# Transposed chunks loaded and split ahead of the tail, the rank ahead of the weight split, low halves of expert weights in two pieces

## What is computed

```python
x = _layernorm(x + attention(x))             # 16 heads, causal
scores = x @ gate_w.T; probs = softmax(scores)
_, idx = top_k(probs + gate_b, 6)            # of E = 16 experts
for each expert:                              # H = 176
    h = silu(x @ W1.T + B1) * (x @ W3.T + B3)
    y += c[:, None] * (h @ W2.T + B2)         # c: prob, 0 if not chosen
z = silu(x @ ws1.T + bs1) * (x @ ws3.T + bs3) @ ws2.T + bs2   # shared, HS = 352
x = _layernorm(x + y + z)
```

## Time and profile before

| | us |
|---|---|
| median of 3 runs | 1126.18 (1124.87 to 1127.89) |
| the profiled execution | 1117.81 |
| its span, first to last instruction | 1115.7 |
| PE busy | 1033.5 (93%) |
| DVE busy | 759.2 (68%) |
| POOL busy | 738.6 (66%) |
| ACT busy | 674.3 (60%) |

### The profile page before, as it was taken

One profiled execution on the slowest core, in us unless ns is written; L12 is line 12 of the kernel. 1 busy time (PEld: TensorE's weight loads), 2 busy tenths in 40 slices (PEclk: granted clock), 3 DMA queues, 4 the chain that ended last, 5 costly groups with the idle time before them and its releaser, 6 DMA issues.

```text
span 1115.7 us, 28318 instructions
## 1 busy us (share of the span) xinstructions
PE 1033.5 (93%) x8028; PEld 845.6 (76%) x8029; DVE 759.2 (68%) x2406; ACT 674.3 (60%) x1680; POOL 738.6 (66%) x671
## 2 busy tenths in 40 slices
PE   7899998989999997798988999999999999999993
PEld 4546564646555553478988999999999999999993
DVE  8786878786878787668756555555555555555467
ACT  3567676767676765755545555555555555555546
POOL 4223368887888888866725666666666666666667
PEclk9999999999999999989999999999999999999997
DMA  6624254545454635466957666777776777777686
GB/s 186 184 75 115 77 141 149 166 143 159 139 172 134 180 128 163 147 214 218 293 162 165 110 117 121 117 117 118 118 120 113 119 119 117 118 117 121 114 238 237
DMA packets 127036, 163.53 MB, mean 147 GB/s; under 512 B 18800, under 2 KB 107504, under 8 KB 126704
## 3 DMA queue, kind: packets, MB, share of 16 engines
q1 hardware_dynamic: 82240, 99.73, 31.0%
q0 software_dynamic: 39024, 54.29, 27.6%
q10 hardware_dynamic: 5696, 8.55, 2.5%
HBM read 65.36 MB, written 73.85 MB: 125 GB/s over the span
## 4 chain that ended last, share of the span: by engine, by line
PE 74%; DVE 12%; ACT 4%; issue 4%; DMA 3%; POOL 2%; SPq 1%; ACTq 0%; POOLq 0%; DVEq 0%
PE psum L1061 18%; PE psum L1088 13%; PE psum L796 10%; PE psum L838 5%; PE psum L826 5%; PE psum L811 4%; PE psum L1046 4%; PE psum L1072 4%; PE psum L1057 3%; DVE rowmax L1501 3%; ACT probs L1164 2%; PE psum L1027 2%; PE psum L813 2%; PE psum L870 1%; DMA stack_q<-shift_l 1%
## 5 line engine op out<-in xcount | busy, mean ns | idle before, releaser
L1164 ACT ACTIVATE probs<-psum 128x512 f32<-128x512 f32 (+2 forms) x384 | 186.4, 529 | 115.8 <-PE psum L826 113.6
L1501 DVE TENSOR_REDUCE rowmax<-psum 128x1 f32<-128x512 f32 (+3 forms) x352 | 212.5, 633 | 60.5 <-PE psum L813 58.1
L2030 POOL DMA_INDIRECT xs_d<-x1p,index x192 | 204.5, 1065 | 52.5 <-issue 45.3
L2098 POOL DMA_INDIRECT x_d<-y_sb,tokens x104 | 162.9, 1566 | 98.6 <-ACT y_sb L1358 48.6
L2098 POOL DMA_INDIRECT z_d<-y_sb,tokens x103 | 161.2, 1565 | 81.4 <-issue 39.4
L1840 DVE TENSOR_TENSOR xb_lo<-psum,xb_hi 128x256 fp32r<-128x256 f32 x207 | 87.9, 425 | 186.2 <-ACT xb_hi L1155 186.2
L1061 PE MATMUL psum<-we_hi_lo,xb_hi 128*128 x828 | 200.6, 323 | 0.0
L1088 PE MATMUL psum<-we_hi_lo,hb_hi 88*128 (+1 forms) x828 | 174.6, 304 | 0.0
L1358 ACT ACTIVATE y_sb<-psum,combine 128x256 f32<-128x256 f32 x207 | 98.4, 475 | 125.0 <-PE psum L1088 112.4
L811 PE MATMUL psum<-stack_k,stack_q 96*128 96x256 bf16 (+3 forms) x512 | 139.0, 311 | 10.9 <-DVE rowmax L1501 4.8
L1061 PEld LDWEIGHTS psum<-we_hi_lo,xb_hi 128*128 128x128 f32 x828 | 146.6, 189 | 0.1
(11 more groups left out here) (206 smaller groups left out, 2326.4 us busy)
## 6 DMA issues: line engine op xcount, KB each, us to landing
xb<-xs_d SPq DMA_DIRECT2D x207, 138.0 KB
stack_q<-q_h SPq DMA_DIRECT2D x48, 128.0 KB
stack_k<-k_h SPq DMA_DIRECT2D x45, 128.0 KB
w_raw<-in_we SPq DMA_DIRECT2D x9, 608.0 KB, 4.4
xT_raw<-in_xT SPq DMA_DIRECT2D x9, 512.0 KB
stack_q<-q_m SPq DMA_DIRECT2D x32, 128.0 KB
stack_k<-k_m SPq DMA_DIRECT2D x32, 128.0 KB
x_res<-in_x SPq DMA_DIRECT2D x8, 512.0 KB, 3.7
```

The lines of the kernel that those rows point to most:

```text
L1164: nc.scalar.activation(probs[kt][:, heads[0]:heads[0] + n, :], st[f % ST_BANKS][:, 0:n * width].rearrange("p (h t) -> p h t", h=n), ACT.Ex ...
L1501: nc.vector.reduce_max(rowmax[gpar][:, heads[0]:heads[0] + n, qt], src, AX.X).then_inc(sm_free, 1)
L2030: nc.gpsimd.indirect_dma_start(out=xs_d[:, :], out_offset=bass.IndirectOffsetOnAxis(ap=index[tp][:, n:n + 1], axis=0), in_=x1p[tp][:, n // ...
L2098: nc.gpsimd.indirect_dma_start(out=(x1_d, z_d)[k % 2][:, :], out_offset=bass.IndirectOffsetOnAxis(ap=tokens[:, k:k + 1], axis=0), in_=y_sb ...
```

## The change

- `W_BY_HALVES_FROM = 6`: from tile 6 on, the low half of an expert is no longer made in its tile T ahead of the epilogue, but in two subtractions of 608 columns, behind the epilogues of tiles T + 1 and T + 2. The rank of tile 12 and the router parts of tile 9 thereby stand ahead of it on DVE. `wt_lo` counts with the second piece.
- Three of the four late chunks (12 to 14) are loaded in blocks 20, 22 and 23, into the memory of `late_raw` and of the first tiles' `hidden`, `h_hi`, `h_lo`, after SP has waited for the last late low half. So a third turn is unrolled (`LATE_TURNS = 3`). Chunk 15 is loaded behind the loop, between the first loads of z and those of x1.
- The late chunks have a buffer each for their halves (`X1T_tail`), and are split at tiles 32, 33, 34 and 38, without a wait for PE. The tail has its own `hidden`, `h_hi`, `h_lo` (`tail_h`), in memory of the first experts.
- `FINAL_FROM = T1 + 6`, `SUMS_AHEAD = 4`: statistics of unit m two tiles sooner, four sums ahead.

```diff
-LATE_TURNS = 2
+LATE_TURNS = 3
...
-FINAL_FROM, SUMS_AHEAD = T1 + 8, 3
+FINAL_FROM, SUMS_AHEAD = T1 + 6, 4
...
+X1T_LATE_AT = {20: 0, 22: 1, 23: 2}
+X1T_SPLIT_AT = {2: 0, 3: 1, 4: 2, 8: 3, 9: 4}
+W_BY_HALVES_FROM = 6
...
+        x1T_late = [sb(f"x1T_late{n}", [P, KD, HT_TOK], where=phase_x) for n in range(len(X1T_LATE_AT))]
+        phase_x.close()
...
+        tail_h = [[sb(f"tail_{name}{n}", [P, HT_TOK], dt) for n in range(2)]
+                  for name, dt in (("hidden", fp32), ("h_hi", f32r), ("h_lo", f32r))]
+        x1T_late += [sb(f"x1T_late{n}", [P, KD, HT_TOK]) for n in range(len(X1T_LATE_AT), HALVES - HC1 - 2)]
...
+        X1T_tail = [sb(f"x1T_tail{n}", [P, 2, KD, HT_TOK], f32r) for n in range(HALVES - HC1 - 2)]
...
+            if T >= T1 + 2:
+                hc = HC1 + 2 + X1T_SPLIT_AT.get(T - T1, HALVES)
+                return hc if hc < HALVES else None
...
-                    if last and k < len(x1T_late):
-                        load_x1T(HC1 + 2 + k)
+                    if isinstance(j0, int) and j0 + k in X1T_LATE_AT:
+                        sp.wait_ge(late_w_lo, 2 * LATE_W)
+                        load_x1T(HC1 + 2 + X1T_LATE_AT[j0 + k])
...
+                if n == 1:
+                    for hc in range(HC1 + 2 + len(X1T_LATE_AT), HALVES):
+                        load_x1T(hc)
...
-                if hc >= 2 and hc != HC1 + 1:
+                if 2 <= hc <= HC1:
                     act.wait_ge(uv_tile_full, ST * (hc - 1))
...
+            def split_half_w(i, half):
+
+                e, cols = W_ORDER[i - ST], slice(half * W_COLS // 2, (half + 1) * W_COLS // 2)
+                if half == 0:
+                    dve.wait_ge(wt_hi, i + 1)
+                last = nc.vector.tensor_tensor(w_all[:, e, 1, cols], w_raw[i % 2][:, cols],
+                                               w_all[:, e, 0, cols].bitcast(fp32), ALU.subtract)
+                if half == 1:
+                    last.then_inc(wt_lo, 1)
...
-                if T in W_ITEM_AT:
+                if T in W_ITEM_AT and T < W_BY_HALVES_FROM:
                     split_w(W_ITEM_AT[T])
...
                 epilogue(T)
+                for half in range(2):
+                    if T - 1 - half in W_ITEM_AT and T - 1 - half >= W_BY_HALVES_FROM:
+                        split_half_w(W_ITEM_AT[T - 1 - half], half)
```

More of the change, by code:

```diff
@@ L244, in postln_layer @@
     phase_a = ExitStack()
-    phase_b, phase_w, phase_z, phase_l = ExitStack(), ExitStack(), ExitStack(), ExitStack()
+    phase_b, phase_w, phase_z, phase_l, phase_x = [ExitStack() for _ in range(5)]
     def sem(name):
@@ L1008, in shared_up @@
                     pe.wait_ge(hidden_done, T - 1)
-                src = X1T[hc % 2]
+                src = x1_halves(hc)
                 for i in range(2):
```

33 lines of the change are left out of this document (17 added, 16 removed).

## The result

The changed kernel takes 1129.54 us in the median of 20 runs (1121.71 to 1138.33), the kernel before 1123.47 us in the median of its 20 beside them (1115.72 to 1127.89). The ratio is 1.0044 with a 95% interval of 1.0026 to 1.0062: **slower by 5 to 6 us**, where 5.3 us faster had been forecast.

What follows compares the result with a forecast made beforehand. TensorE, 74% of the chain, was taken as full inside the loop, leaving three joints: -2.0 - 0.6 - 2.7 = -5.3 us, profiled 1117.81 to 1112.5, plus 8.4 to the median: 1120.9 us, own range 1118.5 to 1123.

Steps and rivals of the forecast that it cites:

- Joint one: Way into the block loop: rank before the weight split 1.8 us, shorter scatters 0.2; -2.0 us, bounds -0.8 and -2.8.
- the loads that wait for the low halves stay covered: Entry: next expert's raw weights load two tiles later, each due three tiles behind the last low half; no cost.
- rival (b): Entry: the loop's start does not move because another wait ends last there; 1122.9 us, chance 0.13.
- the lock: Entry: whole VectorE subtractions hold up GpSimd's scatters, so halving them could bring the entry up to -2.8 us.
- Joint two: Inside the block loop: late loads moved to blocks 20, 22, 23; -0.9 and +0.3, together -0.6 us, bounds -1.1 and +0.6.
- Rival (a): Loop and tail: add backlog not relieved, early statistics eat their gain; tail -0.5, loop +0.3, 1124.0 us, chance 0.20.
- The zero for the unrolled turn: Block loop: saves a loop edge of about 0.1 us, fetches new instructions; 0, bounds -0.2 and +0.6.
- the one for SyncE's wait: Block loop, block 21: SyncE's new wait for late low halves is covered with margin 1.1 us, cost 0.
- Joint three: Way out of the loop, statistics from tile 36 instead of 38: -3.5 + 0.3 + 1.6 - 1.1 = -2.7 us, bounds -4.0 and +0.5.
- -1.1: Tail: TensorE loses its stalls for x1 low halves since every chunk has its own buffer; bounds -0.5 and -1.3 us.
- +0.3 for tiles 46 and 47: Tail: two adds and their statistics moved there bring VectorE to about a tile's length; costs 0.3 us.
- rival (c): Tail: slower, the tile-36 wait lengthened by three loads before the first x1 chunk; tail +3.0, 1127.5 us, chance 0.07.

Runs made afterwards that it cites:

- d_turn: Kernel before with only the third turn of eight blocks unrolled, nothing loaded in it: 0.9991 (0.9961 to 1.0022), median 1120.46 against 1123.01.
- e_order: Kernel before with the rank ahead of the weight split, low half whole in its own tile right behind the rank: 0.9975 (0.9944 to 1.0006).
- w_later: Kernel before with the rank first and the low half whole, two tiles later: 0.9990 (0.9968 to 1.0013).
- u_loads: Changed kernel with only two turns unrolled and the three late-chunk loads back in the last blocks: 1.0018 (0.9994 to 1.0042) against the kernel before.
- d_entry_b: Kernel before with only the rank first and low halves in two pieces one and two tiles later, second run: 1.0018 (0.9991 to 1.0046).
- u_stats: Changed kernel with statistics from tile 38 again and three sums ahead: 1.0031 (0.9993 to 1.0069) against the kernel before, median 1130.96.

## Why the prediction was wrong, point by point

**Joint one, forecast -2.0: the first half held, the sum did not.** In after the first scatter comes 41.3 us behind tile 0 instead of 43.8, the 24 take 30.0 instead of 32.2 (POOL in after; answers to the earlier trace rows):

```profile
527.82 0.95 POOL L2064 DMA_INDIRECT xs_d<-x1p,index  x1 [3.24 <-issue]
...
557.81 0.96 POOL L2064 DMA_INDIRECT xs_d<-x1p,index  x1 [0.30 <-issue]
...
563.83 0.52 POOL L2113 MEMSET hb_hi<- 64x128 f32 x2 [5.06 <-DVE we_hi_lo L1516]
```

Rank: 2.5 sooner, forecast 1.8. Scatters: 2.2 shorter, forecast 0.2. The last scatter ends 4.7 us sooner, and then it is no longer what the clears wait for, but the last expert's low half. The prediction had said that beyond 2.4 us "TensorE would be late next"; it did not ask what TensorE would wait for. The step that failed here is the one sentence that "the loads that wait for the low halves stay covered", a cost put at nothing. It compared due times and not landing times: in after the last load takes 10.2 us to its split instead of 8.8, TensorE stands 2.84 us behind it instead of 1.63, and then runs at the lower clock for some 3.5 us (before has such a stretch too, but behind its wait for the first rows). This is rival (b), by raw weights, and the condition that the prediction had put as its own fall ("if the loop starts where it did"). In the pair of profiles the entry reads -2.1 us, which looked like a hit; the runs of the part alone read 3.8 and 3.9 us slower in the median. With the low half not delayed the forecast's -2.0 is there in the profiles (82.8, 81.9 and 82.6 against 83.8 to 87.5).

The page "SBUF — State Buffer" of the Trainium skill, section "Who interferes with whom", was weighed here. Its remark that a `tensor_tensor` did not stall descriptor writing would have the scatters untouched by VectorE's subtractions; the rows above show them held to the end of each, plus 0.83 us. But the same section has a VectorE instruction with two SBUF inputs contend with a GpSimd instruction that reads SBUF, and these scatters take their row numbers from `index`, a tile in SBUF. The rows agree with that sentence; that the read of `index` is what waits is not shown. Of the prediction's two readings the lock was right in kind; it took 0.2 us for the scatters where 2.2 came.

**Joint two, forecast -0.6: the step that failed first.** "A queue of adds that is behind issues every 4.5 us against 4.64 for two blocks, so it is worked off over some tens of blocks", price at most 0.9. In the profile of after it was (lag 4.7 at block 23, 3.6 at block 39); in the other four profiles with early loads and four buffers it was not, at 6.5 to 8 us each in blocks 24 to 112. The 4.5 us is in before's trace, between adds two blocks apart (4.50, 4.57 and 4.53 us up to blocks 204, 205 and 206), but no row of the prediction shows it, and it was taken to hold whatever waits for the adds. From a lag of about 5 to 5.5 us on (4.8 is the most that a profile in the lower level has in blocks 25 to 55, 5.0 the least in the upper one) the ring of buffers is closed: two blocks then take 4.73 to 4.79 us (208.1 to 210.7 for 88 blocks) and not 4.64, and TensorE goes at the pace of the queue instead of the queue catching up. Rival (a) had named this, "it settles at its upper level after the early loads", but priced it in the tail alone and left the loop at +0.3. The prediction named ScalarE's copies that "wait for adds" in the last blocks, and took it for a short disturbance. The relief of the last blocks did not come: blocks 200 to B take 21.4 instead of 21.2 us, since by then the lag is 5.4 to 6.0 us without any load. The zero for the unrolled turn held within the interval of d_turn, and the one for SyncE's wait held (blocks 16 to 24 in 18.3 us).

**Joint three, forecast -2.7, measured -0.8.** The first terms were right to 0.3 us (DVE, POOL and PE in after):

```profile
1072.45 1.56 POOL L2132 DMA_INDIRECT x_d<-y_sb,tokens  x1 [0.81 <-issue]
...
1081.23 0.75 DVE L1927 BATCH_NORM_STATS2 fin_stats<-fin_x 128x6 f32<-128x256 f32 x2 [3.17 <-POOL fin_x L2143]
1081.90 0.47 DVE L1853 SCALAR_TENSOR_TENSOR tail_hidden<-psum,bias,tail_hidden 128x256 f32<-128x256 f32 x1
...
1084.47 1.77 DVE L1526 TENSOR_TENSOR x1T_tail<-x1T_late,x1T_tail 128x512 fp32r<-128x512 f32 x1
...
1107.13 1.34 DVE L1860 TENSOR_TENSOR tail_h_lo<-tail_hidden,tail_h_hi 128x256 fp32r<-128x256 f32 x1
```
```profile
1082.75 0.50 PE L1049 MATMUL psum<-ws_hi_lo,tail_h_hi 128*128 128x256 f32 x2 [1.79 <-DVE tail_h_lo L1860]
...
1087.81 0.51 PE L1049 MATMUL psum<-ws_hi_lo,tail_h_hi 128*128 128x256 f32 x2 [0.54 <-DVE tail_h_lo L1860]
...
1097.25 0.50 PE L1049 MATMUL psum<-ws_hi_lo,tail_h_hi 128*128 128x256 f32 x2 [0.62 <-DVE tail_h_lo L1860]
...
1105.87 0.50 PE L1049 MATMUL psum<-ws_hi_lo,tail_h_hi 128*128 128x256 f32 x2 [1.23 <-DVE tail_h_lo L1860]
...
1108.53 0.51 PE L1049 MATMUL psum<-ws_hi_lo,tail_h_hi 128*128 128x256 f32 x2 [1.69 <-DVE tail_h_lo L1860]
```

VectorE's wait at tile 36 is 3.17 us (forecast 2.9), tile 37's product B + 15.25 (15.0), TensorE's loss there 1.79 (1.6), and from the last low half to the end 14.8 us instead of 18.6, -3.8 (-3.5). The last add is B + 5.8 and not "about 4 behind".

Two terms failed. The low half of x1 in a buffer of its own still takes 1.77 us at 1084.47, so the long one of the earlier trace rows had not been about buffers: -1.1 was wrong, and TensorE lost 0.54 behind it. What the long ones share is a GpSimd sum (`final_sum`) beside them: behind the loop, in all 18 profiles, a low half of x1 with no sum beside it takes 0.68 to 0.69 us, and only with one beside it does any take 1.65 to 1.81. It is the same for the low halves of the tiles, 0.40 to 0.46 us without a sum and up to 1.54 with one.

The work moved ahead also cost more than "+0.3 for tiles 46 and 47": 0.62 at tile 43, where ScalarE's normalization of 1.09 us now stands before the gated product, and 1.23 + 1.69 at the last two tiles where 0.70 + 1.17 stood before; there the low halves took 0.94 and 1.34 us beside a sum, where before they took 0.42 and 1.37. The last low half comes at B + 40.5 instead of B + 37.5: 3.0 late, 0.8 forecast.

With loads early, late statistics give tails of 55.3, 55.2 and 55.7, early ones 55.3 and 55.8: the statistics moved nothing, rival (a) in its result. What is left of the -0.8 came with the loads and buffers. Without early loads they cost 1 to 3 us (57.7, 57.7 and 58.9 against 55.8 to 56.8): that is rival (c), in those kernels.

**The direction.** Chance of slower 0.07, by rival (c) alone. Slower came otherwise: from a queue with two levels, whose upper one rival (a) named without its price in the loop, and, as far as the profiles tell, from the late raw weights at the entry. Added up, the parts alone agree with the result: loads +2.9 us (0.0026 of 1123), entry +2.0 to +4.8 (0.0018, 0.0043), statistics about 0 (0.9990, interval on both sides): 5 to 8 for 4.9 measured (0.0044). Each of these has an interval of 3 us or more to both sides, so the sum is no proof that nothing is missing; of the two costs, that of the loads is the better shown, that of the entry is in part argued.

**The base.** The prediction carried "8.4 above the profiled one" over to the median and did not ask what made it. 2.7 of them were chance of three runs, since the median of the 20 is 1123.47. Of the other 5.7 the upper level from block 113 on can make all or most (203.6 us against 208.1 to 210.7), which the profiled execution of before alone had escaped; that other executions of before were in it is not shown, since only that one was profiled.

## What to carry to other kernels

A queue that drains in one profile can have two levels that each keep themselves up: look for the buffer that its consumer needs back, count at which lag the ring closes, and do not price a disturbance as one that fades before you have that number. Before arguing in single microseconds, ask what separates the profiled execution from the median; a pair of profiles can agree with the medians in size and disagree in every part. When work is deferred, follow what its completion releases to where it lands, not to where it is due.

## What the runs showed of the hardware

- An indirect scatter on GpSimd that starts inside a VectorE subtraction with both inputs in SBUF is held until the subtraction ends, and ends 0.83 us behind it (67 of 68 scatters in 18 profiles, the last one starting just before the end; 2.11 us instead of 0.96 in the row shown of e_order). Two pieces of 0.78 us hold it for less than one of 1.42 us.
- In the other direction, a VectorE subtraction of 128 x 512 elements takes 0.69 us alone and up to 1.81 us beside a GpSimd addition of two SBUF tiles (48 alone in 18 profiles, all 0.68 or 0.69).
- Behind TensorE's gap at the last raw weights (1.9 to 4.1 us in w_later, after, u_loads, d_entry_b and u_stats) its clock was at 1.2 GHz for 3.5 to 7 us. The gap's length alone does not tell: e_order's wait of 2.8 us for the first rows was not followed by such a stretch.
- In all 18 profiles the lag of the scatter-adds grows by 0.7 to 1.8 us from block 112 to block 113, whatever the kernel. The upper level begins behind this jolt in nine of the ten four-buffer profiles that were not in it before; in that of before, with a jolt of 1.1 us, it does not. The cause of the jolt is open.
- The load of 608 KB of raw weights in a stretch with the DMA engines at a share of about 1.0 takes from 7.2 to 11.4 us from its issue to its split.
